# A macaron block on one core: a later low part and later statistics in the first unit, a third sums bank and earlier numerators in the first stage

## The reference

```python
x = x + 0.5 * (ln(x) @ dequant(qweight).T + bias)      # "quant"
x = x + s4(ln(x), layer 0)                             # "conv": causal convolution along the 512 columns
x = x + 0.5 * (ln(x) @ dequant(qweight).T + bias)      # "quant" again, same weights
x = x + 0.5 * ffn(ln(x))
x = x + s4(ln(x), layer 1)
x = x + 0.5 * ffn(ln(x))                               # the same weights as the ffn above

ffn(y) = (silu(y @ W_gate.T) * (y @ W_up.T)) @ W_down.T   # F = 1376
s4     = irfft(rfft(u) * rfft(K)) + D * u,  K from at_roots = c * (k00 - k01 / (1 + k11) * k10)
```

## Time and profile before

| | us |
|---|---|
| median of 3 runs | 920.38 (916.86 to 920.75) |
| profiled execution | 920.42 |
| its span, first to last instruction | 918.6 |
| TensorE busy | 888.6 (97%) |
| VectorE busy | 619.8 (67%) |
| GpSimd busy | 365.2 (40%) |
| ScalarE busy | 313.5 (34%) |

### The profile page before, as it was taken

The page is one execution under the profiler, slowest core; times in us unless marked ns, Lnnn a source line. Parts: engine busy times, 40 slices in busy tenths (PEclk is TensorE's granted clock), DMA queues, the critical chain, the costliest instruction groups (busy, mean ns, idle before and its releaser), DMA issues.

```text
span 918.6 us, 11736 instructions
## 1 busy us (share of the span) xinstructions
PE 888.6 (97%) x4116; PEld 725.4 (79%) x4116; DVE 619.8 (67%) x1057; ACT 313.5 (34%) x517; POOL 365.2 (40%) x729
## 2 busy tenths in 40 slices
PE   7899999989999999999999999999999999999998
PEld 3777887777777787888888888888888778888876
DVE  7768778788888878555566786655656864544452
ACT  4423446633443444221223352222243512222211
...
PEclk8989999999999999999999999999999999999999
...
DMA packets 41310, 148.27 MB, mean 161 GB/s; under 512 B 3490, under 2 KB 3746, under 8 KB 39844
## 3 DMA queue, kind: packets, MB, share of 16 engines
...
q1 hardware_dynamic: 12212, 46.59, 13.7%
...
...
## 4 chain that ended last, share of the span: by engine, by line
PE 74%; DVE 13%; POOL 7%; issue 2%; DMA 2%; ACT 1%; SPq 0%; DVEq 0%; POOLq 0%; ACTq 0%
PE front L1436 14%; PE front L1438 13%; PE front L1437 13%; PE acc L1390 7%; PE acc L1392 7%; PE acc L1391 7%; PE front L468 3%; DVE weight_operands L600 2%; PE acc L1321 2%; PE acc L1322 2%; PE acc L1320 2%; DVE snapshots L1191 2%; POOL x_rows L748 2%; DVE hidden_lo L1231 2%; POOL rstd L450 1%
## 5 line engine op out<-in xcount | busy, mean ns | idle before, releaser
L1436 PE MATMUL front<-row_operands_hi,weight_operands 128*128 128x512 f32 x616 | 243.2, 395 | 8.2 <-DVE snapshots L1191 8.1
L1438 PE MATMUL front<-row_operands_hi,weight_operands 128*128 128x512 f32 x616 | 240.5, 390 | 0.0
L1437 PE MATMUL front<-row_operands_lo,weight_operands 128*128 128x512 f32 x616 | 240.4, 390 | 0.0
L1436 PEld LDWEIGHTS front<-row_operands_hi,weight_operands 128*128 128x128 f32 x616 | 116.0, 188 | 36.5 <-issue 10.1
L1390 PE MATMUL acc<-down_weights,hidden_hi 128*128 128x512 f32 x352 | 140.0, 398 | 3.9 <-DMA down_weights<-saved_down 2.0
L1191 DVE TENSOR_TENSOR snapshots<-front,snapshots 128x512 f32<-128x512 f32 x132 | 90.9, 689 | 78.3 <-PE front L1438 77.0
L1392 PE MATMUL acc<-down_weights,hidden_lo 128*128 128x512 f32 x352 | 137.4, 390 | 0.0
L1391 PE MATMUL acc<-down_weights,hidden_hi 128*128 128x512 f32 x352 | 137.2, 390 | 0.0
L1438 PEld LDWEIGHTS front<-row_operands_hi,weight_operands 128*128 128x128 f32 x616 | 116.0, 188 | 24.7
L1437 PEld LDWEIGHTS front<-row_operands_lo,weight_operands 128*128 128x128 f32 x616 | 116.1, 189 | 23.3
L820 POOL DMA_DIRECT2D weight_operands<-saved_weights x66 | 48.6, 736 | 185.5 <-PE front L1438 180.6
...
## 6 DMA issues: line engine op xcount, KB each, us to landing
...
x_rows<-x_in SPq DMA_DIRECT2D x3, 1024.0 KB, 11.6
...
```

Of the source, the lines that this page charges most:

```text
L1436: T.matmul(o, wh, xh, start=(j == 0), stop=False)
L1437: T.matmul(o, wh, xl, start=False, stop=False)
L1438: last = T.matmul(o, wl, xh, start=False, stop=(j == 1))
```

## The change

Five edits. (1) `weight_lows` takes the parts to make; in the units the low parts of the raw blocks and of the first sums stay where they were, that of the fourth sum comes behind `second_gate`, and TensorE waits for it ahead of M3 only. (2) In unit 0 the statistics come behind `hidden_lo`. (3) In the first stage the sums go to `acc[0]`, `acc[1]`, `acc[3]` in turn with waits to match, and the transpose of item 4 moves from behind item 0's products to behind item 1's. (4) GpSimd's numerators come before `dequant_lo(0)`, their copies into the right sides after `dequant_lo(1)`; the addition of the squares moves to VectorE, ahead of the first reciprocal. (5) One store of unit 2's rows, issued in unit 3, becomes four.

```diff
--- before.py
+++ after.py
@@ -424,7 +424,7 @@
             l = ITEMS[n].number
             if n >= PRE:
                 return front[3]
-            return acc[l % 2] if l < TILES else acc[(l + 1) % (BLK - 1)]
+            return acc[(0, 1, 3)[l % 3]] if l < TILES else acc[(l + 1) % (BLK - 1)]
 
         def quant_number(n):
 
@@ -593,9 +593,12 @@
             nc.vector.tensor_tensor(raw_block(k, S4), raw_block(k, A12), raw_block(k, S2), ALU.subtract
                                     ).then_inc(w_step, 1)
 
-        def weight_lows(dve, k):
+        RAW, SUMS, FOURTH = range(3)
+
+        def weight_lows(dve, k, parts):
             dve.wait_ge(w_step, 4 * k + 4)
-            for i, (first, last) in enumerate(((A22, A12 + 1), (S2, S3 + 1), (S4, S4 + 1))):
+            for i in parts:
+                first, last = ((A22, A12 + 1), (S2, S3 + 1), (S4, S4 + 1))[i]
                 dve.wait_ge(w_hi, 3 * k + i + 1)
                 nc.vector.tensor_tensor(flat(W, k, LO, first, last), flat(Wr, k, LO, first, last),
                                         flat(W, k, HI, first, last).bitcast(F32), ALU.subtract).then_inc(w_ready, 1)
@@ -683,13 +686,13 @@
                         load_raw(k + 2)
                     if k + 1 < FT:
                         save_weights(k + 1)
-                    if u == 3 and f == 2:
-                        store(2, 1, 0, BLK)
+                    if u == 3 and f in (2, 4, 6, 8):
+                        store(2, 1, f // 2 - 1, f // 2)
                 if u >= 2:
                     store(u, 0, 0, BLK)
             for r in range(BLK):
                 store(3, 1, r, r + 1)
-            sp.wait_ge(stored, 16 * (3 + BLK))
+            sp.wait_ge(stored, 16 * (2 + 2 * BLK))
 
 
         @block.gpsimd
@@ -732,26 +735,7 @@
                 pool.wait_ge(dequant_hi, j + 1)
                 TT(Ql[:, j, :], wq[:, j, :], Qh[:, j, :].bitcast(F32), ALU.subtract).then_inc(dequant_split, 1)
 
-            rstd_step(pool, 0)
-            rstd_step(pool, 1)
-            dequant_lo(0)
-            rstd_step(pool, 2)
-            rstd_step(pool, 3)
-            dequant_lo(1)
-
-            for n in range(XT_SLOTS, RSTD_AHEAD):
-                rstd_step(pool, n)
-
-            def bias_step(n):
-
-                pool.wait_ge(norm_done, n + 1)
-                nc.gpsimd.tensor_tensor(x_tile(ITEMS[n].tile), x_tile(ITEMS[n].tile), biasB[:], ALU.add
-                                        ).then_inc(bias_added, 1)
-
-            NUMERATORS_AT = 1
-
             def numerators():
-
                 pool.wait_ge(b_ready, 1)
                 for a, (ur, ui) in enumerate(((CT_R, CT_I), (Q_R, Q_I))):
                     wide = lambda c: col(c).to_broadcast([P, 2])
@@ -762,7 +746,7 @@
                     TT(num_r[:, a, :], part[:, 0, :], part[:, 1, :], ALU.add)
                     link(TT(num_i[:, a, :], part[:, 2, :], part[:, 3, :], ALU.subtract))
 
-                pool.wait_ge(rstd_ready, NUMERATORS_AT + RSTD_AHEAD + 1)
+            def right_sides():
                 for layer in range(2):
 
                     rows = slice(layer * NS, layer * NS + NS)
@@ -774,6 +758,24 @@
                     TT(rhs2[rows, layer, 4:8], nr, minus[rows, :].to_broadcast([NS, 4]), ALU.mult
                        ).then_inc(numer_ready, 1)
                     pool.wait_ge(numer_ready, (layer + 1) * 4)
+
+            rstd_step(pool, 0)
+            rstd_step(pool, 1)
+            numerators()
+            dequant_lo(0)
+            rstd_step(pool, 2)
+            rstd_step(pool, 3)
+            dequant_lo(1)
+            right_sides()
+
+            for n in range(XT_SLOTS, RSTD_AHEAD):
+                rstd_step(pool, n)
+
+            def bias_step(n):
+
+                pool.wait_ge(norm_done, n + 1)
+                nc.gpsimd.tensor_tensor(x_tile(ITEMS[n].tile), x_tile(ITEMS[n].tile), biasB[:], ALU.add
+                                        ).then_inc(bias_added, 1)
 
             def invert(c):
 
@@ -793,12 +795,6 @@
                     bias_step(n + BIAS_AHEAD)
                 if n >= TILES and n + RSTD_AHEAD < PRE:
                     rstd_step(pool, n + RSTD_AHEAD)
-                if n == NUMERATORS_AT:
-                    numerators()
-                if n == 2:
-
-                    pool.wait_ge(den_squared, 2)
-                    TT(mag[:], mag[:], tmp[:], ALU.add).then_inc(mag_ready, 1)
                 if n in range(4, 4 + KT):
                     invert(n - 4)
                 for later, which in ((3, (0, 1)), (2, (2, 3))):
@@ -1054,6 +1050,9 @@
             def reciprocal(c):
 
                 cols = slice(c * P, (c + 1) * P)
+                if c == 0:
+                    dve.wait_ge(den_squared, 2)
+                    V.tensor_tensor(mag[:], mag[:], tmp[:], ALU.add).then_inc(mag_ready, 1)
                 dve.wait_ge(mag_ready, 1)
                 V.reciprocal(tmp[:, cols], mag[:, cols]).then_inc(den_recip, 1)
 
@@ -1182,7 +1181,7 @@
                 if n == PRE - 5:
                     weight_sums_b(dve, 0)
                 if n == PRE - 3:
-                    weight_lows(dve, 0)
+                    weight_lows(dve, 0, (RAW, SUMS, FOURTH))
 
             def add(k, product, read, out, other):
 
@@ -1248,20 +1247,28 @@
                         weight_sums_b(dve, k + 1)
                     middle_sums_c(k)
                     if k + 1 < FT:
-                        weight_lows(dve, k + 1)
+                        weight_lows(dve, k + 1, (RAW, SUMS))
                     if f == 0 and u:
                         for r in range(BLK):
                             ffn_update(u - 1, 1, r)
                     if 2 <= f < 2 + EMBEDDED[u]:
                         update_step(dve, embedded_item(u, f - 2))
-                    for n in STATS_OF_STEP[u][f]:
-                        stats_step(dve, n)
-                        aggregate_step(dve, n)
+                    if u:
+                        for n in STATS_OF_STEP[u][f]:
+                            stats_step(dve, n)
+                            aggregate_step(dve, n)
                     if 1 <= f <= EMBEDDED[u]:
                         xt_lo_step(dve, embedded_item(u, f - 1))
                     first_hidden(k)
                     second_gate(k)
+
+                    if k + 1 < FT:
+                        weight_lows(dve, k + 1, (FOURTH,))
                     hidden_lo(q, g0)
+                    if u == 0:
+                        for n in STATS_OF_STEP[u][f]:
+                            stats_step(dve, n)
+                            aggregate_step(dve, n)
                 q1 = PASSES * u + FT
                 hidden_lo(q1, H1[:, 0, :])
                 for r in range(BLK):
@@ -1349,9 +1356,9 @@
                     pe.wait_ge(xt_ready, l + 1)
                     if ITEMS[n].kind == "conv":
                         pe.wait_ge(toe_split, ITEMS[n].layer + 1)
-                    if 2 <= l < TILES:
+                    if TILES <= l < TILES + 3:
                         pe.wait_ge(light_updated, l - 1)
-                    if l >= TILES:
+                    elif l >= 3:
                         pe.wait_ge(light_updated, l - 2)
                     products(n)
 
@@ -1360,7 +1367,10 @@
                     pe.wait_ge(toe_ready, 2)
                 if not is_light(user):
                     wait_pair_banks(pe, ITEMS[user].number // 2)
-                if n + XT_AHEAD < PRE:
+
+                if n == 1:
+                    transpose_step(pe, XT_AHEAD)
+                if n and n + XT_AHEAD < PRE:
                     transpose_step(pe, n + XT_AHEAD)
                 if n == 8:
                     cauchy()
@@ -1456,7 +1466,7 @@
                     if f == 0:
                         pe.wait_ge(sums_lo, 4 * BLK * (u + 1))
                     if k < FT:
-                        pe.wait_ge(w_ready, 3 * k + 3)
+                        pe.wait_ge(w_ready, 3 * k + 2)
                     pe.wait_ge(snap_done, k + 1)
                     product(k, M6, S2, T2)
                     pe.wait_ge(front_read, READS * k + C11)
@@ -1477,6 +1487,8 @@
                         pe.wait_ge(w_last_in[k % 2], 16 * ((k - FT) // 2 + 1))
                     pe.wait_ge(front_read, READS * k + T_SUM)
                     product(k, M4, A22, T4N)
+                    if k < FT:
+                        pe.wait_ge(w_ready, 3 * k + 3)
                     pe.wait_ge(front_read, READS * k + C22)
                     product(k, M3, S4, B22)
                     if f == FT - 1:
```

## The result

| | before | after |
|---|---|---|
| median, us | 920.29 (916.86 to 921.81, 6 runs) | 911.53 (906.31 to 913.25, 6 runs) |
| ratio, with its 95% interval | | 0.9906 [0.9885, 0.9928] |
| profiled execution, its span | 920.42, 918.6 | 913.25, 911.5 |

The change gains 8.8 us; 14.6 were forecast. 911.53 lies at the upper edge of the range of 902 to 911.5, just outside it. The profile of after fell on its slowest run, so its span shows 7.1 us of gain.

A forecast was written before the change was run, and what follows sets the result against it. TensorE bounds most of the span, GpSimd's queue the first stage and VectorE's queue the step ends of unit 0. 4.9 + 7.8 + 1.9 = 14.6 us off 920.4 gives 905.8 us, range 902 to 911.5.

The forecast's parts named there:

- GpSimd's queue, 4.9 us: First stage: numerators (3.6 us) and the `mag` addition (1.3) leave GpSimd's queue, so its last inversion comes 4.9 us earlier.
- The whole stretch behind the Cauchy products shifts: From the Cauchy products to unit 0 nothing has a fixed arrival, so stage 1 keeps its full 4.9 us.
- the second rival: Stage 1 gives less: longer gaps before Cauchy and Toeplitz products lose granted clock, 2.3 us in all, 908.1 us; chance 0.09.
- The steps, 7.8 us: Unit 0: `first_hidden`'s addition comes 1.23 us sooner, so eight waits for `snapshots` go, 0.98 us each, 7.8 in all.
- The first rival: Unit 0: GpSimd's `second_hidden` gets ahead of `hidden_lo`, product 5 is 1.25 us late in eight steps; 915.8 us, chance 0.10.
- The last step: Unit 0, steps 9 to 10: no wait there before, so nothing to win.
- Step 0 to 1, 1.9 us: Unit 0: TensorE's gap falls from 2.18 to 1.8 us (0.4 won) and the clock is kept (1.5 won).
- The row of a kept clock at 1.75: A 1.75 us gap at 179.03 left the clock at 1.00; taken as ground for a kept clock in unit 0.
- The save of the weights: Third rival: in unit 0 the later save on SP holds up raw loads, up to 31 us, 936 us; chance 0.04.
- The stores: Unit 3: one store becomes four, TensorE works throughout; 0, at most 0.3 us either way.

The follow-up runs named there:

- after_again: The changed kernel measured once more, with no edit: 912.03 us.
- stage_one_alone: Changed kernel with unit 0's low parts, statistics and waits in their old order, leaving the new first stage and the split store: 914.99 us.
- fourth_alone: Changed kernel with the statistics back ahead of `first_hidden` in unit 0, so only the fourth low part is late there: 914.75 us.
- statistics_alone: Changed kernel with the fourth low part back with the other low parts, so only the statistics are late in unit 0: 910.15 us.
- two_banks: Changed kernel with two sums banks instead of three and item 4's transpose in its old place: 906.23 us.
- last_fourth_early: Changed kernel with the fourth low part of the last step's weights (step 10) back in its old, earlier place: 907.99 us.
- squares_on_gpsimd: Changed kernel with the addition of the squares back in its old place in GpSimd's queue: 910.2 us.
- both_ends: Changed kernel with step 0's first-sums low part behind `second_gate` and the fourth low part of step 10's weights in its old place: 905.89 us.
- first_sums_late: Changed kernel with the low part of the first sums also moved behind `second_gate`, in step 0 of unit 0 alone: 907.47 us.
- idle_filled: Changed kernel with twelve more matmuls, their result overwritten, in TensorE's idle time before the Cauchy products: 907.3 us.

## Why the prediction was wrong

By its steps:

- **GpSimd's queue, 4.9 us**: right (4.75 in after_again). Missed: beside VectorE's instructions that read two SBUF operands its small ones are held up, in three traces of 15 by 1.4 us more, after's among them. Only the reverse was weighed. Why the other 12 traces are spared is open.
- **The whole stretch behind the Cauchy products shifts**: true for the stage alone (from the mark to Toeplitz 50.0 us in stage_one_alone, 54.9 before: 4.9), but not to be relied on. The idle time before them was drawn at 2.5 us and is 3.2, or 4.5 with the hold-ups, and "to Toeplitz" then went anywhere from 18.1 to 21.1: in after_again, fourth_alone and statistics_alone 1.2 us more than before. This is the second rival (chance 0.09), at half its size. What was missed is larger: before is already 3.1 us longer there than a kernel without the gap, where 1.5 were counted for the clock. So TensorE's earlier arrival isn't worth nothing; it costs with the gap open (the third bank, 5.3 to 5.8 us in the medians of two_banks) and pays with the gap filled.
- **The steps, 7.8 us**: right (8.3), in its mechanism too: a step of 12.24 us, `hidden_lo` ahead of `second_hidden`, no wait for `first_gate` or raw weights, and with each part alone steps near the forecast 12.4 and 12.8 (12.45 and 12.9). The first rival did not occur there. The last step, put at nothing, won 0.2.
- **Step 0 to 1, 1.9 us**: gap right (1.79), the 1.5 of the clock mis-sized: lost in five traces of eight with this gap. The row of a kept clock at 1.75 is sound for its own place: all 17 traces have that gap (1.74 to 1.78 us) and keep the clock. It said nothing of another place with 0.04 us more, and was no ground to count the 1.5 in full.
- **The save of the weights**: its cause was seen and followed to the wrong reader. The prediction asked whether the raw loads, 12 us on, would wait for it. It didn't ask who waits for the *last* save, for which no raw load follows: GpSimd's load for step 12. There was no margin before: 330.53 less 319.39 is 11.1 us, and the save landed after 10.6, 0.5 us ahead of the load, as in every trace. The cost is 1.3 to 3.7 us by the segments of the eight traces (2.3 in after; the 3.7 has half clock in it); that it is gone in last_fourth_early shows the cause.
- **The stores**: 0, right ("rest").
- **The end of unit 2**, not in the sum: 1.4 us, in part open. The row of `x_rows` at the top: TensorE waits 0.53 us for it in seven of the eight traces with the late save, and in none of the others. VectorE and GpSimd there, in after:

```profile
698.84 0.69 DVE L1190 TENSOR_TENSOR snapshots<-front,snapshots 128x512 f32<-128x512 f32 x1 [0.25 <-issue]
...
702.08 2.44 DVE L1230 TENSOR_TENSOR hidden_lo<-second_hidden,hidden_hi 128x512 fp32r<-128x512 f32 x1 [0.43 <-ACT hidden_hi L937]
```

```profile
701.94 0.70 POOL L816 DMA_DIRECT2D weight_operands<-saved_weights  x1
702.66 1.30 POOL L837 TENSOR_TENSOR second_hidden<-gate_up 128x512 f32<-128x512 f32 x1
```

and in before:

```profile
710.61 0.69 DVE L1231 TENSOR_TENSOR hidden_lo<-second_hidden,hidden_hi 128x512 fp32r<-128x512 f32 x1 [0.55 <-ACT hidden_hi L941]
```

```profile
710.70 0.70 POOL L820 DMA_DIRECT2D weight_operands<-saved_weights  x1
711.42 1.29 POOL L841 TENSOR_TENSOR second_hidden<-gate_up 128x512 f32<-128x512 f32 x1
```

Before, `hidden_lo` starts 0.09 us ahead of GpSimd's issue of a load and lasts 0.69; after, it starts 0.14 behind that issue and lasts until `second_hidden`, which follows it, has ended: 2.44. The held `hidden_lo` (2.43 to 2.45 us) stands in just the seven traces with the wait for `x_rows`; in the ten others it lasts 0.69. This is the first rival's mechanism, in unit 2. The Trainium skill (SBUF — State Buffer, "SBUF: two separate sides") says that the port pair stays with whichever engine started first for its whole instruction; here the row shows it held over two of GpSimd's (`hidden_lo` began 0.58 us ahead of `second_hidden`). VectorE comes later because it stood still for 0.25 us at 698.84 with "issue" as the reason, again in the seven traces alone. What that is, and how it hangs on a save 390 us earlier, no run here settles; squares_on_gpsimd has the late save without this wait. The rest of this segment is the wait for down weights (1.84 us in after, 1.43 in before) and what follows it: in both_ends, without the late save, "to D" is 2.0 us longer than in before, by a wait of 1.83 and half clock behind it (mean 0.92 from C to D). The same half clock stands in first_sums_late, fourth_alone and idle_filled, the three with "to D" at 23.7 to 23.9.

So the steps of the prediction that failed are the clock from step 0 to 1, the hold-ups of GpSimd, the last save's reader and the end of unit 2. In sum, from the two profiles' segments: 14.6 less 2.4 (stage 1, 1.0 of it the scatter of its start), less 1.6 (step 0 to 1), plus 0.5 (steps), less 2.3 (late save), less 1.4 (unit 2), less 0.2 (rest), is 7.2, and the two spans differ by 7.1. This accounts for one run of each; the medians differ by 8.8.
